# A two-by-two Strassen scheme for w1, and two quadrants added up in PSUM

## The chip, the cores and the metric

The kernel runs on all 8 cores of one Trainium2 chip, each on its own 2048 rows of the input with the same weights; the cores exchange nothing. The time is the device time of the slowest core, in microseconds (us).

## The reference, cut to what matters

```python
xn = _layernorm(x, axis=-1)                       # x: 16384 rows of 1024
s = _L0_attn_ref(xn, input_weights, xis, proj_matrix)
# inside the feed-forward part; _tlin(x, w, s) is (x @ w.T) * s
h = jax.nn.silu(_tlin(x, w1_w, w1_s)) * _tlin(x, w2_w, w2_s)     # 1024 -> 4096, twice
h = jax.nn.gelu(_tlin(h, h1_w, h1_s), approximate=False)         # 4096 -> 4096
h = jax.nn.gelu(_tlin(h, h2_w, h2_s), approximate=False)         # 4096 -> 4096
g = _silu(_tlin(h, w3_w, w3_s))                                  # 4096 -> 1024
x = x + s * g
```

The weights w1, w2, h1, h2 and w3 are ternary (-1, 0, 1); each output column has a scale.

## The kernel before, in words

**Passes and stages.** A core works through two passes (`s_` = 0, 1) of 1024 columns, where a column is one row of x, held transposed. A pass has the stages w12 (w1 and w2 with the gate), h1, h2 and w3; between the passes stands the attention part, which computes s for both. Activations lie in SBUF as bf16 in ten blocks `blk` of 16 tiles of 128 x 512; a tile is 128 features by half of the columns (`th` = 0, 1; N = 512).

**w12 before (`w12_stage`).** 32 chunks, each of 128 features of w1 and the same 128 of w2. For each `th`, `chunk` issues 8 matmuls of w1 into one PSUM bank and 8 of w2 into another, and `gate` has ScalarE write silu of the first to `stg` (L301) and VectorE multiply the second by its scale and by that (L306). Chunk `2*row + half` and `th` give quadrant (half+1, th+1) of the 4096 x 1024 product at `row`: quadrants 11, 12, 21, 22. After two chunks `sums` makes the five sums of quadrants that the next stage reads (L290 to L294). In the first pass `head0` interleaves the layernorm of the second 512 columns with chunks 0 to 6.

**h1, h2, w3 (`hidden_stage`, `row_group`).** These use Strassen's scheme with blocks named 11, 12, 21, 22: seven products M1 to M7 of 16 matmuls each, in the order M2, M5, M1, M4, M7, M3, M6 for each of 16 rows (4 in w3). Bank `bb` holds M2, then M4 is added on top; bank `ba` holds M5, then M3 on top. `ta` collects M1 - M2 - M5. VectorE adds: v1 = bank + ta (L421), then + M7 from a bank of its own (L428) is quadrant 11; v2 (L438), then + M6 from its own bank (L445) is quadrant 22. ScalarE's gelu (L492, L496) or silu follows each. The sums of weights (`weight_sums`, L369, and `sub_in_place`, L376) are made on VectorE during the row before and at the start of the row.

**What sets the order.** Each engine works strictly in the order in which the program issues. `need(engine, tokens)` is a wait; `V` and `S` wait for the instruction before on their own engine too. `take_bank` and `free_bank` hand the 8 PSUM banks round in the order in which they were freed, as the program is written. Weight tiles of 128 x 2048 go through a ring of 8 slots, `wring`; `plan` is the fixed order of loads ("L") and of slots for sums ("S"), and `give_slot` frees a slot once its last matmul is done, on which GpSimd issues the next load.

Of the kernel before, what the change touches and what calls it, by code (L numbers as in the profile page):

```python
# [36 lines left out]
def build_nc():  # L37
# [26 lines left out]
    with contextlib.ExitStack() as stack:  # L64
# [214 lines left out]
        def w12_stage(s_, xnb, bl, after_chunk, head, *toks):  # L279
# [4 lines left out]
            need(v, *toks)  # L284

            def sums(i):

                ops_ready["M2"] = [hv["11", i]]
                ops_ready["M5"] = [hv["22", i]]
                ops_ready["M1"] = [V(lambda: v.tensor_add(kt(bl["M1"], i), kt(h["11"], i), kt(h["22"], i)))]  # L290
                ops_ready["M4"] = [V(lambda: v.tensor_sub(kt(bl["M4"], i), kt(h["21"], i), kt(h["11"], i)))]
                ops_ready["M7"] = [V(lambda: v.tensor_add(kt(h["21"], i), kt(h["21"], i), kt(h["22"], i)))]
                ops_ready["M3"] = [V(lambda: v.tensor_sub(kt(bl["M3"], i), kt(h["12"], i), kt(h["22"], i)))]
                ops_ready["M6"] = [V(lambda: v.tensor_add(kt(h["12"], i), kt(h["12"], i), kt(h["11"], i)))]  # L294

            def gate(i, th, b1, m1, b2, m2):
                row, half = i // 2, i % 2
# [3 lines left out]
                a = S(lambda: sc.activation(stg[:, ts_, :], p[b1], AF.Silu,  # L301
                                            scale=w1s_c[:, oc:oc + 1]),
                      m1, gate_free.get(ts_), now(d_stg[ts_]), col_tok)
                free_bank(b1, a)
                q = str(half + 1) + str(th + 1)
# [36 lines left out]
            first, begun = head(chunk, head_chunks, gate) if head else (0, [])  # L342
            for i in range(first):
                ch = begun[i] if i < len(begun) else chunk(i, 1)
                gate(*ch)
                give_slot(key(i), ch[5])
                if i % 2 == 1:
                    sums(i // 2)
            for i in range(first, 32):
                for th in range(2):  # L350
                    ch = chunk(i, th)
                    gate(*ch)
                give_slot(key(i), ch[5])
                if i % 2 == 1:
                    sums(i // 2)
                after_chunk(i)
# [22 lines left out]
        def row_group(s_, nm, r, bl, nxt, emit, edge):  # L379
# [49 lines left out]
            free_bank(bd, a)  # L429
            t_free[2 * par + 1] = emit("11", r, tb, a)  # L430
# [143 lines left out]
        def head0(chunk, head_chunks, gate):  # L574
# [31 lines left out]
            return 7, ch  # L606

        xn_out = []
        xn_b = b_xn
        first_toks = [[], xn_out]  # L610
        for s_ in range(NS):
            last = s_ == NS - 1

            def after_chunk(i):
# [11 lines left out]
            if not last:  # L626
# [4 lines left out]
                def fetch_edge(u, m):  # L631
# [6 lines left out]
                    elif u == 4:  # L638
                        need(sy, end["u4"], *xn_out)
# [169 lines left out]
                ss = [f32b(b_x)[:, i, :] for i in range(8)] + [f32b(b_q)[:, i, :] for i in range(8)]  # L809
# [14 lines left out]
                first_toks = [[now(d) for d in d_y], [now(d_s)]]  # L824
# [132 lines left out]
```

How the kernel before makes its waits and increments, by code:

```python
    def inc(self, instr, k=1):  # L31
        instr.then_inc(self.sem, k)
        self.n += k
        return (self, self.n)
# [2 lines left out]
def build_nc():  # L37
# [78 lines left out]
        def need(eng, *toks):  # L116
            for tok in toks:
                if tok is None:
                    continue
                ctr, val = tok
                key = (id(eng), id(ctr))
                if val <= 0 or waited.get(key, 0) >= val:
                    continue
                eng.wait_ge(ctr.sem, val)
                waited[key] = val
# [763 lines left out]
                            load(4, [], [end["u6"]])  # L889
                        elif r in (1, 2) and u == 6:
                            load(4 * r + 4, [y_tok[n_] for n_ in range(4 * r - 4, 4 * r)], [])
                    return edge
                for r in range(4):
                    row_group(s_, "w3", r, bl, (s_, "w3", r + 1) if r < 3 else None, emit,
                              edge_load(r))
        for d in d_y:
            sy.wait_ge(d.sem, d.n)
    return nc
```

## Time and profile before

| what | value |
|---|---|
| median of 3 runs | 2374.67 us |
| the profiled execution, its own time | 2374.05 us |
| its span on the slowest core | 2373.0 us |
| TensorE busy, matmuls | 2348.3 us (99%), 10856 |
| VectorE busy | 1139.1 us (48%) |
| ScalarE busy | 416.7 us (18%) |
| mean granted TensorE clock | 0.998 |
| DMA, mean rate | 107 GB/s |

The busy time of an engine is the sum of its instructions; matmuls are pipelined, so that one lasts 379 ns in the records while the next begins some 216 ns after it. "Idle before <-X" is how long an engine stood still, and what X released it.

### The profile page before, as it was taken

The page shows a single profiled execution, that of the slowest core. Times are in us where ns is not written, and L with a number is a line of the kernel's source. Part 1 is how long each engine was busy: PE and PEld are TensorE (multiplying, and loading weights), DVE is VectorE, ACT ScalarE, POOL GpSimd, SP SyncE. Part 2 cuts the span into 40 slices and gives each one's busy share as a digit, 9 for nine tenths or more (in the row PEclk, how much of TensorE's full clock was granted, in tenths as well). Part 3 has the DMA queues.
Part 4 walks back from the last instruction along what each step waited for, and adds up shares of the span by engine and source line. Part 5 has one row for each costly group of instructions (what it writes and reads, how often), then busy time and mean ns, then how long its engine had stood idle before and what let it go on. Part 6 is the DMA issues. An engine that isn't in the chain of part 4 may idle for free.

```text
span 2373.0 us, 30116 instructions; the slowest of 8 cores (2369.7 to 2373.0 us)
## 1 busy us (share of the span) xinstructions
PE 2348.3 (99%) x10856; PEld 1062.3 (45%) x10856; DVE 1139.1 (48%) x1386; ACT 416.7 (18%) x589; POOL 227.9 (10%) x393
## 2 busy tenths in 40 slices
PE   7999999999999999999999999999999999999998
PEld 2444444444444444444444444444444444444443
DVE  4433444444644444463661333444444644444476
ACT  3211111111111111111623112111111111111111
POOL 1100000000100000012040000000000000000000
PEclk9999999999999999999999999999999999999999
DMA  7744456565765656598633443465565756565597
GB/s 108 134 81 71 76 87 107 87 110 91 150 104 95 105 90 111 87 194 136 117 107 103 75 80 63 76 98 102 93 108 89 155 93 108 89 108 92 102 195 201
DMA packets 92307, 253.70 MB, mean 107 GB/s; under 512 B 9856, under 2 KB 28416, under 8 KB 91904
## 3 DMA queue, kind: packets, MB, share of 16 engines
q0 software_dynamic: 57168, 192.96, 51.5%
q1 hardware_dynamic: 34992, 58.81, 7.9%
q8 instruction: 89, 1.46, 0.3%
q14 instruction: 58, 0.48, 0.1%
HBM read 415.31 MB, written 29.36 MB: 187 GB/s over the span
## 4 chain that ended last, share of the span: by engine, by line
PE 96%; DMA 2%; DVE 1%; ACT 0%; issue 0%; POOL 0%; DVEq 0%; ACTq 0%; POOLq 0%
PE pb L157 95%; DMA wring<-w3p 1%; PE pb L335 1%; DMA blk<-xT 0%; PE pb L234 0%; PE pb L235 0%; DVE blk L268 0%; DVE blk L262 0%; DVE blk L306 0%; DVE wring L369 0%; POOL blk L215 0%; DVE blk L860 0%; DVE blk L862 0%; ACT blk L256 0%; DVE blk L243 0%
## 5 line engine op out<-in xcount | busy, mean ns | idle before, releaser
L157 PE MATMUL pb<-blk,wring 128*128 128x512 bf16 x10016 | 2162.7, 379 | 4.5 <-DVE wring L369 2.0
L157 PEld LDWEIGHTS pb<-blk,wring 128*128 128x128 bf16 x10016 | 979.8, 98 | 1187.2 <-issue 6.4
L369 DVE TENSOR_TENSOR wring<-wring 128x2048 bf16<-128x2048 bf16 x216 | 264.6, 1225 | 50.1 <-DVE tmp L445 16.8
L306 DVE SCALAR_TENSOR_TENSOR blk<-pb,cols,stg 128x512 bf16<-128x512 f32 x128 | 96.1, 751 | 268.1 <-PE pb L157 222.0
L376 DVE TENSOR_TENSOR wring<-wring 128x2048 bf16<-128x2048 bf16 x144 | 176.4, 1225 | 15.0
L492 ACT ACTIVATE blk<-pb,cols 128x512 bf16<-128x512 f32 x64 | 44.0, 687 | 664.6 <-DVE tmp L421 664.6
L492 ACT ACTIVATE blk<-tmp,cols 128x512 bf16<-128x512 f32 x128 | 92.4, 722 | 344.0 <-DVE tmp L428 179.8
L301 ACT ACTIVATE stg<-pb,cols 128x512 bf16<-128x512 f32 x128 | 87.9, 687 | 338.4 <-PE pb L157 323.0
L445 DVE TENSOR_TENSOR tmp<-pb,tmp 128x512 f32<-128x512 f32 x72 | 49.8, 692 | 185.4 <-PE pb L157 185.2
L184 POOL DMA_DIRECT2D wring<-h1p x128 | 67.6, 528 | 740.4 <-PE pb L157 740.4
L157 PE MATMUL pb<-blk 128*128 128x512 bf16 x640 | 138.6, 379 | 0.0
L428 DVE TENSOR_TENSOR tmp<-pb,tmp 128x512 f32<-128x512 f32 x72 | 49.8, 692 | 179.3 <-PE pb L157 179.3
L184 POOL DMA_DIRECT2D wring<-h2p x128 | 67.7, 529 | 705.9 <-PE pb L157 673.5
L421 DVE TENSOR_TENSOR tmp<-pb,tmp 128x512 f32<-128x512 f32 x72 | 49.8, 692 | 171.6 <-PE pb L157 170.1
L414 DVE TENSOR_TENSOR tmp<-pb,tmp 128x512 f32<-128x512 f32 x72 | 49.8, 692 | 130.4 <-PE pb L157 129.2
L157 PEld LDWEIGHTS pb<-blk 128*128 128x128 bf16 x640 | 62.6, 98 | 75.5
L438 DVE TENSOR_TENSOR tmp<-pb,tmp 128x512 f32<-128x512 f32 x72 | 49.8, 692 | 88.5 <-PE pb L157 87.6
L496 ACT ACTIVATE stg<-pb,cols 128x512 bf16<-128x512 f32 x64 | 44.0, 687 | 173.4 <-DVE tmp L438 173.4
L184 POOL DMA_DIRECT2D wring<-w12p x64 | 34.2, 542 | 404.1 <-PE pb L157 348.5
L399 ACT COPY tmp<-pb 128x512 f32<-128x512 f32 x72 | 42.2, 586 | 143.9 <-PE pb L157 143.9
L408 DVE TENSOR_TENSOR tmp<-pb,tmp 128x512 f32<-128x512 f32 x72 | 49.8, 692 | 21.6 <-DVE wring L376 16.7
L681 DVE SCALAR_TENSOR_TENSOR tmp<-eb,cols,pb 128x512 f32<-128x512 bf16 x32 | 23.9, 747 | 23.4 <-ACT blk L685 13.8
(72 smaller groups left out, 522.6 us busy)
## 6 DMA issues: line engine op xcount, KB each, us to landing
wring<-h1p POOLq DMA_DIRECT2D x128, 512.0 KB, 7.4
wring<-h2p POOLq DMA_DIRECT2D x128, 512.0 KB, 7.7
wring<-w12p POOLq DMA_DIRECT2D x64, 512.0 KB, 5.9
wring<-w3p POOLq DMA_DIRECT2D x32, 512.0 KB, 10.3
blk<-xT SPq DMA_DIRECT2D x32, 256.0 KB, 8.1
y<-blk SPq DMA_DIRECT2D x32, 256.0 KB, 3.3
blk<-xT POOLq DMA_DIRECT2D x16, 256.0 KB, 22.9
s_hbm<-blk SPq DMA_DIRECT2D x16, 256.0 KB, 2.0
```

Of the source, the lines that this page charges most:

```text
L157: ii = t.matmul(p[bk], lhs, rhs, start=(not onto and i == 0), stop=(i == n - 1), skip_group_check=onto)
L184: toks = d_w[slot].inc(g.dma_start(wring[:, slot, :], src), 16)
L301: a = S(lambda: sc.activation(stg[:, ts_, :], p[b1], AF.Silu, scale=w1s_c[:, oc:oc + 1]), m1, gate_free.get(ts_), now(d_stg[ts_]), col_tok)
L306: a = V(lambda: v.scalar_tensor_tensor(kt(h[q], row), p[b2], w2s_c[:, oc:oc + 1], stg[:, ts_, :], op0=ALU.mult, op1=ALU.mult), m2, a)
L369: tok = V(lambda: v.tensor_add(wring[:, so, :], wring[:, slots[ka][0], :], wring[:, slots[kb][0], :]), *toks, slots[ka][1], slots[kb][1])
L376: tok = V(lambda: v.tensor_sub(wring[:, sa, :], wring[:, sa, :], wring[:, sb_, :]), *toks)
L408: rr = V(lambda: v.tensor_add(ta, p[ba], ta), m, a)
L414: vv = V(lambda: v.tensor_sub(ta, p[bc], ta), m, rr)
L421: v1 = V(lambda: v.tensor_add(tb, p[bb], ta), m, vv, t_free.get(2 * par + 1))
L428: a = V(lambda: v.tensor_add(tb, p[bd], tb), m, v1)
L438: v2 = V(lambda: v.tensor_add(ta, p[ba], ta), m, vv)
L492: a = S(lambda: sc.activation(dst, src, AF.Gelu, scale=s_col[:, oc:oc + 1]), tok, *first_tok)
```

## The change

w1 gets the scheme of the hidden layers: w1 and xn are cut in two by two, and a row (128 features of each half) has seven products of 4 matmuls each, while w2 stays at four plain groups of 8 on the quadrants. The first pass keeps rows 0 to 3 plain (`PLAIN`), the second has all 16 rows in the scheme. Five sums of xn (`input_sums`) and, for each row, five sums of weight tiles (`w12_weight_sums`, three into a slot of their own and two in place) are new work of VectorE. The sums for h1 are made for four rows at once (after rows 4, 8, 12 and 15 begin) and for row 15 at the end. In all layers with the scheme, M7 is now added in the bank of quadrant 21 and M6 in that of 12, after ScalarE has read these; v1 and v2 go, the order becomes M2, M5, M1, M4, M3, M7, M6, and `weight_sums` "s5" moves one unit ahead. The blocks that buffer s between the passes move to others.

```diff
+PLAIN = (4, 0)
...
             for i in range(32):
                 plan.append(("L", (s_, "w12", i, 0), w12p[i]))
+                if i % 2 == 1 and i // 2 >= PLAIN[s_]:
+                    plan.append(("S", (s_, "w12", i // 2, "sum"), None))
...
+        def input_sums(xnb, bl):
+            xn = wide(xnb)
+            b11, b12 = xn[:, 0:4, 0:N], xn[:, 0:4, N:2 * N]
+            b21, b22 = xn[:, 4:8, 0:N], xn[:, 4:8, N:2 * N]
+            at = lambda i: blk[:, bl["out11"] if i < 4 else bl["out22"],
+                               i % 4 * 2048:(i % 4 + 1) * 2048].rearrange("p (k c) -> p k c", k=4)
+            xs = {"M2": b11, "M5": b22, "M1": at(0), "M4": at(1), "M7": at(2), "M3": at(3), "M6": at(4)}
+            V(lambda: v.tensor_add(xs["M1"], b11, b22))
+            V(lambda: v.tensor_sub(xs["M4"], b21, b11))
+            V(lambda: v.tensor_sub(xs["M3"], b12, b22))
+            V(lambda: v.tensor_add(xs["M7"], b21, b22))
+            tok = V(lambda: v.tensor_add(xs["M6"], b11, b12))
+            return xs, tok
+        def w12_weight_sums(s_, r):
+            (sa, ta_), (sb, tb_) = slots[s_, "w12", 2 * r, 0], slots[s_, "w12", 2 * r + 1, 0]
+            so, toks = slots[s_, "w12", r, "sum"]
+            a11, a12 = wring[:, sa, 0:N], wring[:, sa, N:2 * N]
+            a21, a22 = wring[:, sb, 0:N], wring[:, sb, N:2 * N]
+            out = lambda i: wring[:, so, i * N:(i + 1) * N]
+            V(lambda: v.tensor_add(out(0), a21, a22), *toks, ta_, tb_)
+            V(lambda: v.tensor_add(out(1), a11, a12))
+            V(lambda: v.tensor_add(out(2), a11, a22))
+            V(lambda: v.tensor_sub(a12, a12, a22))
+            slots[s_, "w12", r, "sum"] = (so, V(lambda: v.tensor_sub(a21, a21, a11)))
...
+            def sums(i0, i1):
+                rows = lambda b: blk[:, b, i0 * N:(i1 + 1) * N]
+                ops_ready["M2"] = [hv["11", i1]]
+                ops_ready["M5"] = [hv["22", i1]]
+                ops_ready["M1"] = [V(lambda: v.tensor_add(rows(bl["M1"]), rows(h["11"]), rows(h["22"])))]
...
+            def row_plain(first):
+                ch = head(chunk, head_chunks, gate)
+                for i in range(first):
+                    c = ch[i] if i < len(ch) else chunk(i, 1)
+                    gate(*c)
+                    give_slot(key(i), c[5])
+                for i in range(first, 2 * PLAIN[s_]):
+                    for th in range(2):
+                        c = chunk(i, th)
+                        gate(*c)
+                    give_slot(key(i), c[5])
+            def row(r):
+                par = r % 2
+                ta, tb = tmp[:, 2 * par, :], tmp[:, 2 * par + 1, :]
+                ka, kb, ks = key(2 * r), key(2 * r + 1), (s_, "w12", r, "sum")
+                def unit(bk, kw, k0, op, onto=False):
+                    need(t, slots[kw][1])
+                    return mm_group(bk, [(wtile(kw, k0 + k), xs[op][:, k, :]) for k in range(4)], onto)
+                def plain(q):
+                    kw = kb if q[0] == "2" else ka
+                    cs = slice(0, N) if q[1] == "1" else slice(N, 2 * N)
+                    bk = take_bank()
+                    return bk, mm_group(bk, [(wtile(kw, 8 + k), xn[:, k, cs]) for k in range(8)])
+                bb = take_bank()
+                m = unit(bb, ks, 0, "M2")
+                copy_tok = S(lambda: sc.copy(ta, p[bb]), m, t_free.get(2 * par))
+                ba = take_bank()
+                m = unit(ba, ks, 4, "M5")
+                rr = V(lambda: v.tensor_add(ta, p[ba], ta), m, copy_tok)
+                if r < 15:
+                    w12_weight_sums(s_, r + 1)
+                z21 = plain("21")
+                bc = take_bank()
+                m = unit(bc, ks, 8, "M1")
+                give_slot(ks, m)
+                vv = V(lambda: v.tensor_sub(ta, p[bc], ta), m, rr)
+                free_bank(bc, vv)
+                for i0, i1 in ((0, 3), (4, 7), (8, 11), (12, 14)):
+                    if r == i1 + 1:
+                        sums(i0, i1)
+                z12 = plain("12")
+                need(t, copy_tok)
+                m = unit(bb, kb, 4, "M4", onto=True)
+                g21 = silu(1, r, p[bb], m)
+                z11 = plain("11")
+                need(t, rr)
+                m = unit(ba, ka, 0, "M3", onto=True)
+                g12 = silu(0, r, p[ba], m)
+                z22 = plain("22")
+                product("21", r, *g21, *z21)
+                after_row(r, 0)
+                product("12", r, *g12, *z12)
+                after_row(r, 1)
+                need(t, g21[1])
+                m = unit(bb, ka, 4, "M7", onto=True)
+                give_slot(ka, m)
+                a = V(lambda: v.tensor_add(tb, p[bb], ta), m, vv, t_free.get(2 * par + 1))
+                free_bank(bb, a)
+                g11 = silu(0, r, tb, a)
+                t_free[2 * par + 1] = g11[1]
+                need(t, g12[1])
+                m = unit(ba, kb, 0, "M6", onto=True)
+                give_slot(kb, m)
+                a = V(lambda: v.tensor_add(ta, p[ba], ta), m)
+                free_bank(ba, a)
+                g22 = silu(1, r, ta, a)
+                t_free[2 * par] = g22[1]
+                product("11", r, *g11, *z11)
+                product("22", r, *g22, *z22)
+                after_row(r, 2)
+            if head:
+                row_plain(7)
+                xs, xs_tok = input_sums(xnb, bl)
+                w12_weight_sums(s_, PLAIN[s_])
+            else:
+                xs, xs_tok = xs
+            need(t, xs_tok)
+            for r in range(PLAIN[s_], 16):
+                row(r)
+            sums(15, 15)
...
             m = unit(bb, "a22", "M4", onto=True)
             give_slot(key("a22"), m, slots[key("a12")][1])
-            v1 = V(lambda: v.tensor_add(tb, p[bb], ta), m, vv, t_free.get(2 * par + 1))
-            free_bank(bb, emit("21", r, p[bb], v1))
+            out21 = emit("21", r, p[bb], m)
             edge_(3, m)
-            bd = take_bank()
-            m = unit(bd, "a12", "M7")
-            give_slot(key("a12"), m)
-            a = V(lambda: v.tensor_add(tb, p[bd], tb), m, v1)
-            free_bank(bd, a)
-            t_free[2 * par + 1] = emit("11", r, tb, a)
+            need(t, rr)
+            m = unit(ba, "a11", "M3", onto=True)
+            give_slot(key("a11"), m, slots[key("a21")][1])
+            out12 = emit("12", r, p[ba], m)
             if nxt:
                 weight_sums(*nxt, "s2")
             edge_(4, m)
-            need(t, rr)
-            m = unit(ba, "a11", "M3", onto=True)
-            give_slot(key("a11"), m, slots[key("a21")][1])
-            v2 = V(lambda: v.tensor_add(ta, p[ba], ta), m, vv)
-            free_bank(ba, emit("12", r, p[ba], v2))
+            need(t, out21)
+            m = unit(bb, "a12", "M7", onto=True)
+            give_slot(key("a12"), m)
+            a = V(lambda: v.tensor_add(tb, p[bb], ta), m, vv, t_free.get(2 * par + 1))
+            free_bank(bb, a)
+            t_free[2 * par + 1] = emit("11", r, tb, a)
+            if nxt:
+                weight_sums(*nxt, "s5")
             edge_(5, m)
-            be = take_bank()
-            m = unit(be, "a21", "M6")
+            need(t, out12)
+            m = unit(ba, "a21", "M6", onto=True)
             give_slot(key("a21"), m)
-            a = V(lambda: v.tensor_add(ta, p[be], ta), m, v2)
-            free_bank(be, a)
+            a = V(lambda: v.tensor_add(ta, p[ba], ta), m)
+            free_bank(ba, a)
             t_free[2 * par] = emit("22", r, ta, a)
             if nxt:
-                weight_sums(*nxt, "s5")
...
-                if i >= 29:
-                    weight_sums(s_, "h1", 0, ("s2", "s5", "s1")[i - 29])
-            w12_stage(s_, xn_b, bl, after_chunk, None if s_ else head0, *first_toks[0])
+            def after_row(r, i):
+                if r == 15:
+                    weight_sums(s_, "h1", 0, ("s2", "s5", "s1")[i])
...
-                ss = [f32b(b_x)[:, i, :] for i in range(8)] + [f32b(b_q)[:, i, :] for i in range(8)]
+                ss = [f32b(fr2)[:, i, :] for i in range(8)] + [f32b(fr1)[:, i, :] for i in range(8)]
+                bl = {"M2": b_sq, "M5": b_wt, "M1": b_f, "M4": fr1, "M7": fr2, "M3": fr3,
+                      "M6": b_iw, "out11": b_x, "out22": b_q, "out21": b_xn1}
+                xs_next = input_sums(b_xn1, bl)
+                w12_weight_sums(1, 0)
...
-                first_toks = [[now(d) for d in d_y], [now(d_s)]]
-                bl = {"M2": b_sq, "M5": b_wt, "M1": b_f, "M4": fr1, "M7": fr2, "M3": fr3,
-                      "M6": b_iw, "out11": b_x, "out22": b_q, "out21": b_xn1}
+                first_toks = [[now(d) for d in d_y] + [now(d_s)], []]
...
-                order = [(("21", "11", "12", "22")[k], r) for r in range(4) for k in range(4)]
+                order = [(("21", "12", "11", "22")[k], r) for r in range(4) for k in range(4)]
...
-                            load(0, [end["u4"]], [end["u5"], now(d_s)])
+                            load(0, [end["u5"]], [now(d_s)])
```

## Rows read from the trace of the kernel before

**Rows 1.** waits of TensorE, whole span: total us, times, longest

```profile
PE pb L335 <- DVE blk L268: 6.1, 1, 6.1
...
PE pb L157 <- DVE wring L369: 2.0, 2, 1.3
...
PE pb L157 <- ACT stg L301: 1.6, 1, 1.6
```

**Rows 2.** windows of h1 and the second w12, columns in its first line

```profile
core 6: us, PE busy (x) PEld busy (x) DVE busy (x) ACT busy (x) POOL busy (x), PEclk, DMA share, GB/s
257.00:644.00 387.00, 387.00 (x1795) 175.45 (x1794) 186.83 (x211) 55.74 (x81) 33.83 (x64) 1.00 0.61 104
...
1273.00:1495.00 222.00, 222.00 (x1031) 100.64 (x1029) 81.77 (x141) 45.84 (x66) 14.84 (x28) 1.00 0.40 69
```

**Rows 3.** the chain that ended last: start us, length us, what

```profile
22.78 7.18 PE pb L335 x24
...
1054.58 1.24 DVE wring L369
1055.81 0.14 issue
...
1190.79 1087.81 PE pb L157 x5040
```

**Rows 4.** windows of 2 us around TensorE's longest idle time

```profile
16.00:18.00 2.00, 0.67 (x4) 0.10 (x1) 1.12 (x2) 0.44 (x1) 0.00 (x0) 1.00 1.06 160
18.00:20.00 2.00, 0.00 (x0) 0.00 (x0) 1.72 (x3) 0.44 (x2) 0.00 (x0) 0.93 1.01 152
...
24.00:26.00 2.00, 2.00 (x6) 0.76 (x5) 1.90 (x2) 0.00 (x0) 0.00 (x0) 0.50 1.11 145
26.00:28.00 2.00, 2.00 (x9) 0.83 (x8) 1.79 (x3) 1.18 (x2) 0.00 (x0) 0.87 1.27 171
```

**Rows 5.** groups by form, VectorE and ScalarE: busy us, mean ns | idle before

```profile
L369 DVE TENSOR_TENSOR wring<-wring 128x2048 bf16<-128x2048 bf16 x216 | 264.6, 1225 | 50.1 <-DVE tmp L445 16.8 <-DVE tmp L428 16.4 <-DMA wring<-w3p 8.1
...
L306 DVE SCALAR_TENSOR_TENSOR blk<-pb,cols,stg 128x512 bf16<-128x512 f32 x128 | 96.1, 751 | 268.1 <-PE pb L157 222.0 <-ACT stg L301 35.0 <-DVE blk L294 6.8
...
L301 ACT ACTIVATE stg<-pb,cols 128x512 bf16<-128x512 f32 x128 | 87.9, 687 | 338.4 <-PE pb L157 323.0 <-PE pb L335 11.7 <-DVE blk L290 2.8
...
L408 DVE TENSOR_TENSOR tmp<-pb,tmp 128x512 f32<-128x512 f32 x72 | 49.8, 692 | 21.6 <-DVE wring L376 16.7 <-PE pb L157 5.0
...
L262 DVE TENSOR_TENSOR blk<-blk 128x1024 f32<-128x1024 bf16 x8 | 9.8, 1225 | 0.8
...
L290 DVE TENSOR_TENSOR blk<-blk 128x512 bf16<-128x512 bf16 x32 | 13.6, 425 | 3.3
```

**Rows 6.** timeline of VectorE, first w12: start us, length us, what

```profile
45.65 0.75 DVE L306 SCALAR_TENSOR_TENSOR blk<-pb,cols,stg 128x512 bf16<-128x512 f32 x1 [0.17 <-DVE blk L306]
...
245.59 0.75 DVE L306 SCALAR_TENSOR_TENSOR blk<-pb,cols,stg 128x512 bf16<-128x512 f32 x1 [0.24 <-PE pb L157]
...
254.30 0.75 DVE L306 SCALAR_TENSOR_TENSOR blk<-pb,cols,stg 128x512 bf16<-128x512 f32 x1 [2.70 <-PE pb L157]
255.15 0.42 DVE L290 TENSOR_TENSOR blk<-blk 128x512 bf16<-128x512 bf16 x1
255.68 0.43 DVE L291 TENSOR_TENSOR blk<-blk 128x512 bf16<-128x512 bf16 x1
```

**Rows 7.** DMA issues of the page: KB, median us to landing

```profile
wring<-h1p POOLq DMA_DIRECT2D x128, 512.0 KB, 7.4
...
wring<-w12p POOLq DMA_DIRECT2D x64, 512.0 KB, 5.9
wring<-w3p POOLq DMA_DIRECT2D x32, 512.0 KB, 10.3
```

**Rows 8.** timeline of VectorE, end of the program

```profile
2367.39 0.69 DVE L445 TENSOR_TENSOR tmp<-pb,tmp 128x512 f32<-128x512 f32 x1 [0.17 <-DVE blk L862]
...
2369.87 0.69 DVE L862 TENSOR_TENSOR blk<-blk 128x512 f32<-128x512 f32 x1
```

More of the change, by code:

```diff
@@ L276, in ln_extra, with w12_stage @@
                                              op0=ALU.mult, op1=ALU.mult), ln[th, "rstd"])
-        def w12_stage(s_, xnb, bl, after_chunk, head, *toks):
+        def input_sums(xnb, bl):
[22 more added lines that the diff above has]
+            slots[s_, "w12", r, "sum"] = (so, V(lambda: v.tensor_sub(a21, a21, a11)))
+        def w12_stage(s_, xnb, bl, xs, after_row, head, *toks):
             xn = wide(xnb)
@@ L283, in w12_stage, with silu @@
             gate_n = [0]
[L284 to L297, printed above, removed]
+            def sums(i0, i1):
[3 more added lines that the diff above has]
+                ops_ready["M1"] = [V(lambda: v.tensor_add(rows(bl["M1"]), rows(h["11"]), rows(h["22"])))]
+                ops_ready["M4"] = [V(lambda: v.tensor_sub(rows(bl["M4"]), rows(h["21"]), rows(h["11"])))]
+                ops_ready["M3"] = [V(lambda: v.tensor_sub(rows(bl["M3"]), rows(h["12"]), rows(h["22"])))]
+                ops_ready["M7"] = [V(lambda: v.tensor_add(rows(h["21"]), rows(h["21"]), rows(h["22"])))]
+                ops_ready["M6"] = [V(lambda: v.tensor_add(rows(h["12"]), rows(h["12"]), rows(h["11"])))]
+            def silu(half, row, src, tok):
                 oc = half * 16 + row
@@ L300, in gate, with product @@
                 gate_n[0] += 1
[L301 to L305, printed above, removed]
+                return ts_, S(lambda: sc.activation(stg[:, ts_, :], src, AF.Silu,
+                                                    scale=w1s_c[:, oc:oc + 1]),
+                              tok, gate_free.get(ts_), now(d_stg[ts_]), col_tok)
+            def product(q, row, ts_, a, b2, m2):
+                oc = (int(q[0]) - 1) * 16 + row
                 a = V(lambda: v.scalar_tensor_tensor(
                     kt(h[q], row), p[b2], w2s_c[:, oc:oc + 1], stg[:, ts_, :],
-                    op0=ALU.mult, op1=ALU.mult), m2, a)
+                    op0=ALU.mult, op1=ALU.mult), m2, a, *toks)
                 gate_free[ts_] = a
@@ L311, in gate @@
                 hv[q, row] = a
+            def gate(i, th, b1, m1, b2, m2):
+                row, half = i // 2, i % 2
+                ts_, a = silu(half, row, p[b1], m1)
+                free_bank(b1, a)
+                product(str(half + 1) + str(th + 1), row, ts_, a, b2, m2)
             key = lambda i: (s_, "w12", i, 0)
@@ L340, in head_chunks @@
                         for i in range(n)] if jj == 3 else None
[L342 to L356, printed above, removed]
+            def row_plain(first):
[9 more added lines that the diff above has]
+                    give_slot(key(i), c[5])
@@ L605, in head0 @@
             xn_out.append(d_xn.inc(sy.dma_start(xn_hbm, blk[:, b_xn, :]), 16))
-            return 7, ch
+            return ch
         xn_out = []
         xn_b = b_xn
+        xs_next = None
         first_toks = [[], xn_out]
@@ L612, in build_nc @@
             last = s_ == NS - 1
-            def after_chunk(i):
-                if i >= 29:
-                    weight_sums(s_, "h1", 0, ("s2", "s5", "s1")[i - 29])
-            w12_stage(s_, xn_b, bl, after_chunk, None if s_ else head0, *first_toks[0])
+            def after_row(r, i):
+                if r == 15:
+                    weight_sums(s_, "h1", 0, ("s2", "s5", "s1")[i])
+            w12_stage(s_, xn_b, bl, xs_next, after_row, None if s_ else head0, *first_toks[0])
             bl = hidden_stage(s_, "h1", bl, h1s_c, "h2", first_toks[1])
@@ L638, in fetch_edge @@
                     elif u == 4:
-                        need(sy, end["u4"], *xn_out)
+                        need(sy, end["u5"], *xn_out)
                         fetched["xn"] = d_xn.inc(sy.dma_start(blk[:, fr3, :], xn_hbm), 16)
```

## The prediction

> **What bounds the kernel now.** I read the waits of TensorE first: the whole span holds few, and the longest (6.1 us) lie in the layernorm of the head; of the long middle there is 2.0 us for sums of w3's weights [rows 1]. Then the windows by stage: TensorE is busy for all 387.0 us of h1 and for all 222.0 us of the second w12, at a clock of 1.00 [rows 2]. Then the chain that ended last, which names one piece of 1087.81 us with 5040 matmuls, 0.2158 us each [rows 3]. So the time is the number of matmuls times 0.2158 us plus holes, and any hole that the change opens in front of TensorE counts in full. VectorE has room today: 81.77 of 222 us, 37%, in w12 [rows 2].
>
> **What it removes.** A row of w1 and w2 costs 64 matmuls today (two halves, two `th`, 16 each) and 7*4 + 4*8 = 60 then. There are 12 such rows in the first pass and 16 in the second: 28*4 = 112 matmuls, 112*0.2158 = **24.2 us less**, if they run back to back. A row then lasts 60*0.2158 = 12.95 us. In the hidden layers the count stays; 144 adds of VectorE go (v1 and v2, 72 rows, 0.69 us each by the like of [rows 5]), some 100 us of its work, but TensorE never waited for them there: nothing.
>
> **What it adds: a hole after the plain rows.** In the first pass `input_sums` stands behind the last plain gate in VectorE's order, and `row(4)` can't begin before it and before `w12_weight_sums`. Nothing is queued for TensorE meanwhile. Price: the last product 0.75 [rows 5] and its start, 0.8; five adds of 2048 bf16 elements, for which the nearest row is the weight sum of the same size, 1.225 [rows 5], and 0.10 to the next one (425 ns long, 0.53 from start to start [rows 6]), 5*1.33 = 6.65; five adds of 512, 5*0.53 = 2.65; 0.14 to TensorE [rows 3]. Together **10.3 us**. The operands of `input_sums` are four runs of 512 and not one run of 2048: if that halves the rate, as for the float32 centering that takes 1225 ns for 1024 elements [rows 5], an add takes 2.29 us and the hole is 5.3 us longer. I take the fast figure since the inner run is contiguous as in the rows at 425 ns. The Trainium skill (VectorE: DVE Perf Modes, What auto-detection actually checks) asks for 16-bit tensors with a step of one for the double rate; by it the hole stays at 10.3 us, and no row here has this very form.
>
> **And the clock.** Before the 6.1 us wait of today the clock was 1.00; the window 18:20 shows a mean of 0.93, so it fell near 19.9, and it came back in 26:28 (0.87), some 3.5 us after the matmuls had restarted at 22.78 (the figure before the last two of each window's line is the clock, columns as in [rows 2]) [rows 4]. The 24 matmuls there took 7.18 us [rows 3] where 24*0.2158 is 5.18: the fall costs **2.0 us**. The new hole is longer, so I add it once in full.
>
> **A hole before h1, in both passes.** h1's first product needs quadrant 11 of row 15, which today is long done. In the new order VectorE makes it after both late adds. I count from the start of row 15, from the durations in [rows 5] with the lags of [rows 6] (0.17 before one that reads PSUM behind another, 0.24 behind or before a weight sum): the row before leaves an add and two products, so rr ends at 3.45; vv follows M1 (4.32) and ends at 5.1; the sums of rows 12 to 14 are five adds of 1536 (0.96 each, between 425 for 512 and 1225 for 2048) with 0.10 between, to 10.4; product 21 to 11.4; s2 of h1 to 12.9; product 12 to 13.8; s5 to 15.3; the add after M7 to 16.3; that after M6 to 17.1; product 11 to 18.1; TensorE at 18.2. It had finished at 12.95: **5.25 us, twice, 10.5 us**. Product 22, s1 and the last sums follow under M2's 3.45 us and M5's. Bounds: 3.5 us each if the lags are smaller and s5 comes ahead of its turn, 7 if a load holds s5. Does the clock fall in 5.25 us? The only fall known is at 6.1 us; I take half of 2.0 for each, **2.0 us** together, with 0 and 4.0 as bounds. The Trainium skill (TensorE: Matmul & The Clock Gate, Why this matters for your kernels) warns of idle gaps between bursts; it would have the clock fall in all three holes, which makes 4.0 of these 2.0.
>
> **Small waits inside the rows.** Each row takes 7 of 8 banks, so a bank is needed again one row later. In rows 4, 8 and 12 of the program VectorE has five adds of 2048 more: rr to 3.45, weight sums to 6.2, vv to 7.2, the stage sums to 13.8, product 21 to 14.8, and its bank is wanted at 12.95 + 1.73 = 14.7. I take 0.3 us, six times, **2 us**; 0 and 9 us are the bounds (below). In other rows VectorE catches up.
>
> **What is hidden.** The second pass's `input_sums` and first weight sums (9.3 us) run under the 128 matmuls of s (27.6 us). M7 now waits for ScalarE to have read quadrant 21, and M6 for 12: some 0.7 us each [rows 5], and a table load once in a stage, under 16 matmuls of 3.45 us. "s5" is now wanted 10.4 us after its load is issued, which lands in 7.4 us in h1 [rows 7]; where it is later (w3, 10.3 us) VectorE stands, with the add after M6 behind it, but TensorE needs s5 only 3.45 us later, and that wait is today's 2.0 us [rows 1]. The loads of w12 are issued some 16 us before their sums and land in 5.9 us [rows 7]. Fetches and spills keep their place by units. At the end, VectorE starts its last PSUM add at 2367.39, held up by the add before it, and ends at 2370.56 [rows 8]; with one add less it is some **0.3 us** earlier.
>
> **Sum.** 2374.05 - 24.2 + 10.3 + 2.0 + 10.5 + 2.0 + 2 - 0.3 = 2376.4 for the profiled execution; the median of the runs is 0.6 above that execution, so **2377 us**, 0.1% more than today. A measurement of this kernel can tell about 2% from no change.
>
> **Rivals.**
> (1) *The holes are covered*: the sums run ahead of where I place them, and only the matmuls count: 2374.7 - 24.2 = 2350 us. For it: VectorE is 63% idle in w12. Against: its order is the program's, and a product of the last plain chunk stands in front of the sums. 0.07.
> (2) *VectorE paces the w1 rows*, the case on the slower side. Its work per row with lags: rr 0.9, weight sums 2.9, vv 0.9, four products 3.7, two adds 1.7, a quarter of the stage sums 1.7, together 11.8 of 12.95 us, 91% instead of 37%. It decides from 0.07 us more for each of the 16 instructions of a row on. Then the six bank waits grow from 0.3 to some 1.5 us (+7) and each hole before h1 by 1 us (+2): 2386. If the bf16 adds ran at half rate in all places, each row would be 1.4 us over: 28 of them and the longer hole give 2420; the 425 ns rows speak against that. 0.18.
> (3) *The input sums run at half rate and the clock falls in all three holes*: 2377 + 5.3 + 2 = 2384 us. For it: the strided form is not in the trace. Against: the contiguous runs of 512. 0.12.
> The forecast, the holes as priced, has 0.60; 0.03 is for something that I don't see, more likely slower.
>
> **Range.** Low end: small lags (-3.5), no fall of the clock before h1 (-2) nor after the plain rows (-2), no bank waits (-2), a little of the first hole: 2366. High end: rivals (2) and (3) with most of their price: 2390. It leaves out rival (1) and the tails, under 0.15. Faster by over 2% would need 47 us, which no case gives: 0.01; slower by as much only the extreme form of (2): 0.03; within 2% 0.96.
>
> **What would show it.** TensorE: 10744 matmuls instead of 10856; one wait of some 10 us before the first scheme row, near 88 us, for a VectorE weight sum, with the clock at half behind it; one of some 5 us before h1 at about 257 and 1491 us for a product of VectorE; waits of a few tenths for bank releases three times in each w12; none within h1 and h2. Input sums at 1.23 us (or 2.29, rival 3). VectorE's share in the second w12 near 75%. I am wrong if the waits before h1 are absent or TensorE waits in every row.

## The result, and the profile after

The changed kernel takes 2380.17 us (median of 12 undisturbed executions) against 2374.78 us (14): ratio 1.0022, 95% interval 1.0014 to 1.003, so 5.4 us slower and within 2%. The forecast was 2377 us, 2366 to 2390. The profiled execution took 2378.95 us, its span is 2377.9 us on core 4. Disturbed executions, in which the cores of a die ran at a lower granted clock, are left out of all medians and ratios here (with them the two medians are 2380.64 and 2374.9 us); on one chip some at 20 us above the rest stayed in and made three intervals wide, where the profiles are the better reading. The kernels ran on several chips, and the kernel before has medians of 2374.24 to 2374.84 us on them, so a difference between kernels of two chips is good to some 0.6 us.

The page of the changed kernel, its engines and two of its groups of instructions (busy us, mean ns of one | idle before them):

```profile
PE 2332.0 (98%) x10744; PEld 1052.1 (44%) x10744; DVE 1170.8 (49%) x1394; ACT 435.2 (18%) x617; POOL 229.3 (10%) x393
...
L158 PE MATMUL pb<-blk,wring 128*128 128x512 bf16 x9904 | 2145.3, 380 | 27.2 <-DVE blk L338 12.5
...
L338 DVE SCALAR_TENSOR_TENSOR blk<-pb,cols,stg 128x512 bf16<-128x512 f32 x128 | 96.1, 751 | 71.2 <-ACT stg L332 35.4
```

TensorE has 10744 matmuls instead of 10856. Its busy time fell by 16 us and not by the 24.2 us of 112 matmuls, since some of the others now run at a lowered clock, as shown below. VectorE has 32 us more, though 144 adds went from the hidden layers. The idle time of TensorE ahead of its main group is 27.2 us; it was 4.5 us on the page of the kernel before.

The waits of TensorE in the changed kernel answer to [rows 1]:

```profile
PE pb L158 <- DVE blk L338: 12.5, 7, 5.7
PE pb L158 <- DVE wring L309: 10.5, 1, 10.5
PE pb L373 <- DVE blk L271: 6.1, 1, 6.1
...
PE pb L158 <- DVE wring L478: 1.5, 2, 1.2
```

The first two are new: 12.5 us for products of VectorE (L338 is `product` and `gate`) in seven waits, and 10.5 us in one piece for the last of the weight sums (L309). In the timeline of TensorE each stretch without a wait is one line; the bracket is the wait before it:

```profile
67.12 20.88 PE L158 MATMUL pb<-blk,wring 128*128 128x512 bf16 x96
98.51 68.56 PE L158 MATMUL pb<-blk,wring 128*128 128x512 bf16 x308 [10.50 <-DVE wring L309]
167.69 4.48 PE L158 MATMUL pb<-blk,wring 128*128 128x512 bf16 x20 [0.62 <-DVE blk L338]
172.35 47.64 PE L158 MATMUL pb<-blk,wring 128*128 128x512 bf16 x220 [0.18 <-issue]
220.26 37.34 PE L158 MATMUL pb<-blk,wring 128*128 128x512 bf16 x172 [0.27 <-DVE blk L338]
262.73 803.02 PE L158 MATMUL pb<-blk,wring 128*128 128x512 bf16 x3712 [5.12 <-DVE blk L338]
...
1284.47 66.64 PE L158 MATMUL pb<-blk,wring 128*128 128x512 bf16 x308
1351.38 52.02 PE L158 MATMUL pb<-blk,wring 128*128 128x512 bf16 x240 [0.28 <-DVE blk L338]
1403.67 52.02 PE L158 MATMUL pb<-blk,wring 128*128 128x512 bf16 x240 [0.27 <-DVE blk L338]
1455.96 37.35 PE L158 MATMUL pb<-blk,wring 128*128 128x512 bf16 x172 [0.27 <-DVE blk L338]
1498.96 802.77 PE L158 MATMUL pb<-blk,wring 128*128 128x512 bf16 x3712 [5.65 <-DVE blk L338]
```

The reader finds here the hole after the plain rows (10.50 us), the holes before h1 (5.12 and 5.65 us) and six waits of 0.18 to 0.62 us within w12. No line breaks inside h1 or h2: 3712 matmuls follow one another. A record shows a matmul as 0.38 us long while the next starts 0.216 us after it, so each wait is 0.16 us longer than its bracket says: 96 matmuls at 0.2158 us are 20.72 us, the record of the first line has 20.88.

VectorE in the first hole, from its timeline (start us, length us):

```profile
88.18 0.75 DVE L338 SCALAR_TENSOR_TENSOR blk<-pb,cols,stg 128x512 bf16<-128x512 f32 x1 [2.70 <-PE pb L158]
89.04 1.23 DVE L291 TENSOR_TENSOR blk<-blk 128x2048 bf16<-128x2048 bf16 x1
...
97.94 0.42 DVE L309 TENSOR_TENSOR wring<-wring 128x512 bf16<-128x512 bf16 x1
```

The last plain product (L338) is followed by the five input sums (L291 to L295), each 1.22 or 1.23 us long, and by the five weight sums (L305 to L309), each 0.42 us long. VectorE's load over most of the second w12 answers to the second line of [rows 2], in the same columns:

```profile
1285.00:1492.00 207.00, 206.18 (x954) 92.75 (x952) 143.83 (x219) 54.63 (x80) 15.98 (x30) 1.00 0.46 78
```

It is busy for 143.83 of 207 us, 69%, where it was 37% before.

The clock after the first hole, in windows of 2 us (columns as in [rows 2], the clock third from the end; they answer to [rows 4]):

```profile
90.00:92.00 2.00, 0.00 (x0) 0.00 (x0) 1.79 (x3) 0.00 (x0) 0.00 (x0) 1.00 0.88 131
92.00:94.00 2.00, 0.00 (x0) 0.00 (x0) 1.90 (x2) 0.00 (x0) 0.00 (x0) 0.55 0.73 104
98.00:100.00 2.00, 1.49 (x4) 0.58 (x5) 0.36 (x1) 0.00 (x0) 0.00 (x0) 0.50 0.00 0
102.00:104.00 2.00, 2.00 (x10) 0.85 (x9) 1.40 (x3) 0.00 (x0) 0.00 (x0) 0.89 0.04 8
260.00:262.00 2.00, 0.00 (x0) 0.00 (x0) 1.55 (x3) 0.96 (x2) 0.00 (x0) 1.00 0.97 133
262.00:264.00 2.00, 1.27 (x4) 0.56 (x5) 1.72 (x3) 0.48 (x1) 0.00 (x0) 0.71 0.66 129
...
266.00:268.00 2.00, 2.00 (x10) 0.94 (x9) 1.69 (x4) 0.00 (x0) 0.00 (x0) 0.93 0.00 0
```

It fell in the hole near 92 and came back after 102; before h1 it fell at about 262.8, just as the wait ended, and came back after 266, and near 1498.5, in the hole before the second h1, once more. Thus 308 matmuls after the first hole lasted 68.56 us where the same stretch takes 66.64 us at full clock (the experiment with the input sums in the head has it), 1.9 us more. The stretch of 3712 matmuls behind the second hole took 803.02 us against 801.33 us at full clock (seen in the experiments with z22 last and with the filled holes), 1.7 us more, and behind the third 802.77, 1.4 us more.

VectorE before the third hole, from its timeline (start us, length us, idle before):

```profile
1489.83 0.96 DVE L326 TENSOR_TENSOR blk<-blk 128x1536 bf16<-128x1536 bf16 x1
1490.96 0.75 DVE L338 SCALAR_TENSOR_TENSOR blk<-pb,cols,stg 128x512 bf16<-128x512 f32 x1 [0.17 <-DVE blk L326]
1491.95 1.23 DVE L478 TENSOR_TENSOR wring<-wring 128x2048 bf16<-128x2048 bf16 x1 [0.24 <-DVE blk L338]
1493.42 0.75 DVE L338 SCALAR_TENSOR_TENSOR blk<-pb,cols,stg 128x512 bf16<-128x512 f32 x1 [0.24 <-PE pb L158]
1494.41 1.23 DVE L478 TENSOR_TENSOR wring<-wring 128x2048 bf16<-128x2048 bf16 x1 [0.24 <-DVE blk L338]
1496.16 0.69 DVE L441 TENSOR_TENSOR tmp<-pb,tmp 128x512 f32<-128x512 f32 x1 [0.53 <-DVE wring L478]
1497.03 0.69 DVE L448 TENSOR_TENSOR tmp<-pb,tmp 128x512 f32<-128x512 f32 x1 [0.17 <-DVE tmp L441]
1498.06 0.75 DVE L338 SCALAR_TENSOR_TENSOR blk<-pb,cols,stg 128x512 bf16<-128x512 f32 x1 [0.34 <-ACT stg L332]
```

This is the chain that the prediction worked out: the last stage sum, product 21, s2, product 12, s5, the adds behind M7 and M6, product 11. TensorE had finished w12 by 1493.3 us and waits for the last of these lines.

### The profile page after: what moved, and what is told of

Read it like the earlier page. It is cut to its first block, busy times and chain, and to the rows that moved or that the text cites. A ratio compares the mean times of both kernels' runs of the same rounds, so it can differ in the third digit from the quotient of the medians.

```text
span 2377.9 us, 30054 instructions; the slowest of 8 cores (2374.2 to 2377.9 us)
## 1 busy us (share of the span) xinstructions
PE 2332.0 (98%) x10744; PEld 1052.1 (44%) x10744; DVE 1170.8 (49%) x1394; ACT 435.2 (18%) x617; POOL 229.3 (10%) x393
## 4 chain that ended last, share of the span: by engine, by line
PE 92%; DVE 4%; DMA 2%; issue 1%; ACT 0%; DVEq 0%; POOL 0%; ACTq 0%; POOLq 0%
PE pb L158 91%; DMA wring<-w3p 1%; PE pb L373 1%; DVE blk L338 1%; DMA blk<-xT 0%; DVE blk L322 0%; DVE blk L326 0%; DVE blk L323 0%; DVE blk L325 0%; DVE blk L324 0%; PE pb L237 0%; PE pb L238 0%; DVE wring L478 0%; DVE blk L271 0%; DVE blk L265 0%
## 5 line engine op out<-in xcount | busy, mean ns | idle before, releaser
L158 PE MATMUL pb<-blk,wring 128*128 128x512 bf16 x9904 | 2145.3, 380 | 27.2 <-DVE blk L338 12.5
L158 PEld LDWEIGHTS pb<-blk,wring 128*128 128x128 bf16 x9904 | 969.1, 98 | 1203.1 <-issue 41.5
L545 DVE TENSOR_TENSOR tmp<-pb,tmp 128x512 f32<-128x512 f32 x72 | 49.8, 692 | 365.5 <-PE pb L158 364.6
L523 DVE TENSOR_TENSOR tmp<-pb,tmp 128x512 f32<-128x512 f32 x72 | 49.8, 692 | 171.0 <-PE pb L158 170.1
L338 DVE SCALAR_TENSOR_TENSOR blk<-pb,cols,stg 128x512 bf16<-128x512 f32 x128 | 96.1, 751 | 71.2 <-ACT stg L332 35.4
L555 DVE TENSOR_TENSOR tmp<-pb,tmp 128x512 f32<-128x512 f32 x72 | 49.8, 692 | 85.2 <-PE pb L158 84.2
L517 DVE TENSOR_TENSOR tmp<-pb,tmp 128x512 f32<-128x512 f32 x72 | 49.8, 692 | 74.8 <-PE pb L158 73.1
L332 ACT ACTIVATE stg<-pb,cols 128x512 bf16<-128x512 f32 x72 | 49.5, 687 | 191.0 <-PE pb L158 178.4
L605 ACT ACTIVATE stg<-pb,cols 128x512 bf16<-128x512 f32 x64 | 44.0, 687 | 177.2 <-PE pb L158 177.2
L332 ACT ACTIVATE stg<-tmp,cols 128x512 bf16<-128x512 f32 x56 | 40.4, 722 | 111.0 <-DVE tmp L441 106.6
L791 DVE SCALAR_TENSOR_TENSOR tmp<-eb,cols,pb 128x512 f32<-128x512 bf16 x32 | 23.9, 748 | 24.5 <-ACT blk L795 15.7
L795 ACT ACTIVATE blk<-tmp,bias_f,cols 128x512 bf16<-128x512 f32 x32 | 26.0, 813 | 45.5 <-DVE tmp L791 45.4
## 6 DMA issues: line engine op xcount, KB each, us to landing
wring<-w3p POOLq DMA_DIRECT2D x32, 512.0 KB, 10.3
```

Source lines behind the costliest of these rows:

```text
L158: ii = t.matmul(p[bk], lhs, rhs, start=(not onto and i == 0), stop=(i == n - 1), skip_group_check=onto)
L332: return ts_, S(lambda: sc.activation(stg[:, ts_, :], src, AF.Silu, scale=w1s_c[:, oc:oc + 1]), tok, gate_free.get(ts_), now(d_stg[ts_]), ...
L338: a = V(lambda: v.scalar_tensor_tensor(kt(h[q], row), p[b2], w2s_c[:, oc:oc + 1], stg[:, ts_, :], op0=ALU.mult, op1=ALU.mult), m2, a, *toks)
L517: rr = V(lambda: v.tensor_add(ta, p[ba], ta), m, a)
L523: vv = V(lambda: v.tensor_sub(ta, p[bc], ta), m, rr)
L545: a = V(lambda: v.tensor_add(tb, p[bb], ta), m, vv, t_free.get(2 * par + 1))
```

## The experiments

Kernels that ran together share their runs of the kernel before; ratios are to that.

### Input sums in the head

```diff
             ln_extra(1)
+            early.append(input_sums(b_xn, bl))
             need(sy, ln[1, "xn", 3])
...
                         c = chunk(i, th)
+                        if (i, th) == (2 * PLAIN[s_] - 1, 1):
+                            w12_weight_sums(s_, PLAIN[s_])
                         gate(*c)
...
-                xs, xs_tok = input_sums(xnb, bl)
-                w12_weight_sums(s_, PLAIN[s_])
+                xs, xs_tok = early[0]
```

> The five sums of xn are made in the head, right after the layernorm of the second 512 columns, and the first weight sums ahead of the last plain gate. Theory (each hole in front of TensorE counts in full, and the clock falls behind it): the wait of 10.5 us for a weight sum goes, and the 2.1 us of half clock behind it, so 12.6 us less than the changed kernel: 2368 us, ratio to the kernel before 0.997. Rival (the hole is only moved: the sums now hold up the gates of chunks 0 to 2, banks run short in the head): half of it comes back, 2374 us, ratio 1.000, with a new wait of TensorE between 60 and 75 us.

Measured: 2368.24 us, ratio 0.9981 (0.9965 to 0.9998). The timeline of TensorE in this kernel, at the same places:

```profile
67.69 20.88 PE L158 MATMUL pb<-blk,wring 128*128 128x512 bf16 x96
88.98 66.64 PE L158 MATMUL pb<-blk,wring 128*128 128x512 bf16 x308 [0.40 <-DVE wring L309]
```

The hole shrank from 10.50 to 0.40 us, the 308 matmuls behind it take 66.64 us, and nothing new stands in the head. Against the 2380.2 us of the changed kernel that is 11.9 us; 12.6 were expected. The hole was a matter of order alone.

### Row 15 reordered

```diff
-                for i0, i1 in ((0, 3), (4, 7), (8, 11), (12, 14)):
+                for i0, i1 in ((0, 3), (4, 7), (8, 11), (12, 13)):
...
+                if r == 15:
+                    after_row(r, 0)                  # s2 of h1
+                    product("21", r, *g21, *z21)
...                                                   # M7, its add, M6, its add, as before
+                    z22 = plain("22")
+                    product("11", r, *g11, *z11)
+                    product("22", r, *g22, *z22)
+                    after_row(r, 1)                  # s5
+                    product("12", r, *g12, *z12)
+                    after_row(r, 2)                  # s1
+                    return
...
-            sums(15, 15)
+            sums(14, 15)
```

> Only row 15 of w12 is reordered: z22 is issued last on TensorE, h1's first weight sum comes before product 21, s5 behind product 22, and the stage sums of rows 12 and 13 are made in row 14, those of 14 and 15 at the end. Theory: the waits of 5.1 and 5.7 us before h1 fall under 0.5 us each and the clock no longer falls there (2.1 us each): some 14 us less than the changed kernel, 2366 us, ratio 0.996. Rival (VectorE has too much work at this place, and TensorE meets the same backlog some units later, at h1's M3, which needs an add of VectorE): 2372 us, ratio 0.999, with waits of some 2 us within h1's first row.

Measured: 2366.41 us, ratio 0.9997 (0.997 to 1.0024). Of the nine executions six lie at 2365.5 to 2366.7 us, among them the profiled one (2366.41), and three at 2386.4 to 2386.7. The ratio is inconclusive, the profile is not: TensorE's stretch from row 13 into h1, h2 and up to w3 is now one line in each pass.

```profile
220.38 839.04 PE L158 MATMUL pb<-blk,wring 128*128 128x512 bf16 x3884 [0.27 <-DVE blk L338]
...
1449.58 839.04 PE L158 MATMUL pb<-blk,wring 128*128 128x512 bf16 x3884 [0.62 <-DVE blk L338]
```

3884 matmuls at 0.2158 us are 838.3 us, so there is neither a wait nor a lowered clock of more than 0.6 us in them. The median of the lower six, 2365.9 us, is 14.3 us under the changed kernel; 14 were expected. The backlog does not come back within h1's first row.

### The holes filled with matmuls

```diff
+            def keep_busy(n):
+                i, tok = banks.popleft()
+                need(t, tok)
+                for _ in range(n):
+                    t.matmul(p[i], ones_d, xn[:, 0, 0:N], start=True, stop=True)
+                banks.appendleft((i, None))
...
                 row_plain(7)
+                keep_busy(46)
...
+            keep_busy(22)
             sums(15, 15)
```

> The changed kernel with matmuls that compute nothing of use in its three holes: 46 after the plain rows (9.9 us) and 22 before each h1 (4.7 us). The holes keep their length. Theory (the 6.4 us that the sum of matmuls, waits and holes leaves over is the clock at half behind each hole): the clock stays at 1.00 outside the head, 6.3 us less than the changed kernel, 2374 us, ratio 1.000. Rival (what is left over lies in the hidden layers or in w12's rows, and the lowered clock is only shown, not paid): 2380 us, ratio 1.002.

Measured: 2373.9 us, ratio 1.0011 (0.9979 to 1.0043), which can't tell 6 us, so the kernel ran again beside the changed one:

> The changed kernel itself, on the same chip as the next kernel, since the filled holes left an interval of 0.9979 to 1.0043 that can't tell 6 us. Both theories: ratio 1.0022 to the kernel before, 2380 us.

Measured: 2380.46 us, ratio 1.0022 (1.0012 to 1.0033).

> The kernel with the three holes filled by matmuls once more, beside the changed kernel. Theory (the clock at half behind the holes costs 5.2 to 6.3 us in all): 2374.5 us, 6 us less than the changed kernel, mean clock 0.998 on all cores against 0.994. Rival (the lowered clock is shown, not paid): the same time as the changed kernel within 1 us.

Measured: 2374.24 us, ratio 0.9998 (0.9989 to 1.0008); the intervals don't touch. The clock in the windows of the first filled kernel:

```profile
88.00:98.00 10.00, 9.70 (x45) 4.21 (x43) 8.82 (x11) 0.00 (x0) 0.53 (x1) 1.00 0.31 52
98.00:104.00 6.00, 5.73 (x27) 2.67 (x28) 2.96 (x8) 0.58 (x1) 0.00 (x0) 1.00 0.00 0
...
258.00:263.00 5.00, 4.63 (x23) 1.94 (x21) 4.27 (x6) 1.44 (x2) 0.00 (x0) 1.00 0.60 105
```

The waits for VectorE's results ended when they did before (0.57 us of wait behind 9.9 us of added matmuls, where 10.50 us of wait stood), only the clock stayed at 1.00. So some 6.2 us of the changed kernel's time (2380.46 - 2374.24) are the lowered clock. One core's records give 1.9 + 1.7 + 1.4 = 5.0 us; the time of eight cores is that of the slowest, and the falls differ from core to core (the 308 matmuls behind the first hole took 68.0 to 69.5 us on the eight cores of the repeated run).

### The two halves of the change apart

The first kernel is the one before with `row_group` of the changed one (and the waits at the passages that go with it), the second the changed one with `row_group` of before.

> The kernel before with the second half of the change alone: M7 and M6 are added up in the banks of 21 and 12 in h1, h2 and w3, w12 stays plain. Theory (TensorE never waited for the adds that go, and the new waits for ScalarE are covered by a unit of 3.45 us): ratio 1.000, within 1 us of the kernel before, some 100 us less work on VectorE. Rival (the new waits for ScalarE and the earlier s5 cost TensorE something in each of 72 rows): 5 us more, ratio 1.002.

Measured: 2373.26 us, ratio 0.9994 (0.9985 to 1.0004). VectorE's busy time fell from 1139.1 to 1038.4 us:

```profile
PE 2337.0 (99%) x10639; PEld 1062.5 (45%) x10856; DVE 1038.4 (44%) x1242; ACT 416.7 (18%) x589; POOL 228.4 (10%) x393
```

The count of TensorE has missing records here (10639 of 10856). A hundred microseconds of VectorE went, and the time did not move by what can be told.

> The changed w12, with the hidden layers as they were (M7 and M6 in banks of their own, order M2, M5, M1, M4, M7, M3, M6). Theory: w12 alone makes the whole difference to the kernel before, and the two halves add up: 2374.5 + 6 from w12, some 1 us above the changed kernel, 2381 us, ratio 1.003. Rival (w12 profits from the banks that the hidden layers no longer take, or the two disturb each other at the passage to h1): the wait before h1 differs by over 1 us from the 5.1 and 5.7 us of the changed kernel.

Measured: 2380.84 us, ratio 1.0026 (1.0015 to 1.0038), with waits of 10.50, 5.13 and 5.29 us. w12 alone makes the difference, and (2380.84 - 2374.41) + (2373.26 - 2374.24) is 5.5 us, near the 5.4 us of both: the halves add up.

### Stage sums split over two rows

```diff
                     if r == i1 + 1:
-                        sums(i0, i1)
+                        sums(i0, i1, 0 if i1 < 12 else 2)     # 0: M1, M4, M3
+                    elif r == i1 + 2 and i1 < 12:
+                        sums(i0, i1, 1)                       # 1: M7, M6
```

> The five stage sums of four rows are made in two rows: M1, M4, M3 in rows 4, 8, 12 and M7, M6 one row later. Theory (the waits of 0.27 to 0.62 us for a product of VectorE are bank waits caused by the 6.65 us of sums before it): these go, holes as before, 1.9 us less than the changed kernel, 2379 us, ratio 1.0015. Rival (they come from VectorE's average load, not from the lump): they stay or move to the next row, 2380.6 us.

Measured: 2377.83 us, ratio 1.0014 (1.0002 to 1.0025). TensorE runs the whole of the second w12 in one line:

```profile
1284.54 207.36 PE L158 MATMUL pb<-blk,wring 128*128 128x512 bf16 x960
```

The waits within w12 are gone, in the first pass too (one stretch of 720 matmuls there), and with them the one of 0.18 us that the record puts to no one. The 2.3 us by the medians is within what two intervals leave open; that the waits are gone is seen.

### Two adds more in each row

```diff
             V(lambda: v.tensor_add(out(0), a21, a22), *toks, ta_, tb_)
+            V(lambda: v.tensor_add(out(0), a21, a22))
             V(lambda: v.tensor_add(out(1), a11, a12))
+            V(lambda: v.tensor_add(out(1), a11, a12))
```

> The changed kernel with two of the five weight sums of each w1 row made twice: two adds of 512 elements, 1.06 us of VectorE, more in each of 28 rows. Theory (VectorE is 90% busy there but has room except behind the stage sums): the six bank waits grow by 1.05 us each, the hole after the plain rows by 1.06 us: 7.4 us more, 2388 us, ratio 1.0055. Rival (VectorE already paces the rows, as I held possible): each of the rows pays 1.06 us, 28 us more, 2409 us, ratio 1.0145.

Measured: 2387.0 us, ratio 1.0052 (1.0032 to 1.0072). The waits within the second w12 (some matmuls are missing from the counts):

```profile
1357.10 51.80 PE L158 MATMUL pb<-blk,wring 128*128 128x512 bf16 x235 [1.33 <-DVE blk L340]
1410.45 52.01 PE L158 MATMUL pb<-blk,wring 128*128 128x512 bf16 x236 [1.55 <-DVE blk L340]
1463.79 37.34 PE L158 MATMUL pb<-blk,wring 128*128 128x512 bf16 x168 [1.33 <-DVE blk L340]
```

This is core 6, where the changed kernel shows 0.27, 0.49 and 0.27 us at these places (some records are missing on core 6 of both kernels; cores with all of them show 1.33 us against 0.27). Each grew by the 1.06 us added, the two waits for products in the first pass likewise (1.32 and 1.33 us), the hole after the plain rows went from 10.50 to 11.56 us, and no other row waits. By the medians it is 6.8 us more than the changed kernel; 7.4 were expected, 28 by the rival. VectorE is close to pacing these rows, but does so only behind the lump of stage sums.

### Two steps of the reorder alone

In the first kernel s5 is called after product 22 in row 15. In the second z22 is last on TensorE as above, but the stage sums of rows 12 to 14 stay in row 15 and s2 behind product 21.

> Of the reorder of row 15 only one step: h1's weight sum s5 goes behind product 22 in both passes. Theory (the wait before h1 is VectorE's queue, each entry at its full length): the waits shrink by 1.5 and 1.8 us to 3.6 and 3.8 us. If the clock still falls behind them: 3.3 us less than the changed kernel, 2377 us, ratio 1.001. If it no longer falls: 7.5 us less, 2373 us, ratio 0.999. Rival (the wait is set by something else, such as silu of quadrant 11): waits unchanged, 2380.6 us.

Measured: 2377.78 us, ratio 1.001 (0.9998 to 1.0022); waits of 3.65 and 4.01 us.

> In row 15 the plain group z22 is issued last on TensorE, and s5 and product 12 come behind product 22; the stage sums of rows 12 to 14 stay in row 15 and s2 stays behind product 21. Theory by VectorE's queue: the add after M7 starts 13.1 us into the row, product 11 ends at 15.6, TensorE finished at 12.95: waits of 2.8 us, no fall of the clock, 9 us less than the changed kernel, 2372 us, ratio 0.9985. Rival (eight matmuls at the end cover the whole queue, as in the full reorder): waits under 0.5 us, 2366 us, ratio 0.996.

Measured: 2372.24 us, ratio 0.999 (0.998 to 1.0001); waits of 2.44 and 2.60 us. Both fit VectorE's queue within 0.4 us. On the clock I was wrong: behind 2.44 us it fell on two of the eight cores, and behind 2.60 us on four. Windows of cores 1 and 6 of the second kernel, the same stretch:

```profile
259.00:261.00 2.00, 0.54 (x2) 0.28 (x3) 1.59 (x3) 1.07 (x2) 0.09 (x1) 0.89 0.63 61
261.00:263.00 2.00, 2.00 (x6) 0.66 (x5) 1.65 (x3) 0.00 (x0) 0.00 (x0) 0.50 1.00 201
```

```profile
259.00:261.00 2.00, 0.98 (x5) 0.51 (x6) 1.50 (x2) 0.72 (x1) 0.00 (x0) 1.00 0.58 84
261.00:263.00 2.00, 2.00 (x11) 0.87 (x9) 1.79 (x2) 0.00 (x0) 0.00 (x0) 1.00 0.90 178
```

The 3712 matmuls behind it took 803.02 us on core 1 and 801.33 us on core 6. With s5 late, too, core 7 kept its full clock behind the wait of 4.01 us while core 6 lost it. The time is that of the slowest core, and so near the 2377 us expected for s5 late with falls, not the 2373 us without.

### All three mends together

> The early sums of xn, the reordered row 15 and the split stage sums together. Theory: what is left is 112 matmuls less and about 1.1 us from the hidden layers, with under 1 us of waits: 2374.5 - 24.2 - 1.1 + 1 = 2350 to 2353 us, ratio 0.990. Rival (the parts share a gain, as where VectorE's work put off in one place fills another): under two thirds of it, 2358 us or more, ratio over 0.993.

Measured: 2350.53 us, ratio 0.9899 (0.9882 to 0.9916): 23.9 us less than the kernel before, clock 0.997 to 0.998 on all cores. Waits of TensorE, then its timeline from the second w12 to the end:

```profile
PE pb L375 <- DVE blk L271: 6.1, 1, 6.1
...
PE pb L158 <- DVE wring L507: 0.9, 1, 0.9
PE pb L158 <- DVE wring L309: 0.4, 1, 0.4
```

```profile
1264.95 1078.13 PE L158 MATMUL pb<-blk,wring 128*128 128x512 bf16 x4992
```

The second pass runs from w12 to the last matmul, 4992 of them, without a wait. The parts were worth 11.9, 14.3 and 2.3 us alone, 28.5 in sum, and 29.6 us together: no gain is shared that the medians could tell.

## Why the prediction was right, point by point

- **Matmuls, -24.2 us.** Held: 10744, and units of four on changing banks ran at 0.2158 us each like all others. The version with all mends gains 23.9 us, which is this term and little else.
- **The hole after the plain rows, 10.3 us.** 10.50 by the record. Its five sums took 1.23 us each, the fast figure; the half-rate part of rival 3 is out. The rule of the Trainium skill (VectorE: DVE Perf Modes, What auto-detection actually checks) fits these rows: 16-bit tensors in runs with a step of one, at 1.23 us for 2048 elements and not 2.29.
- **The clock after it, 2.0 us.** 1.9. The 2.0 was read from a record that is itself 0.16 us too long, so the fall in the head had cost 1.8.
- **The holes before h1, 10.5 us.** 5.12 and 5.65, so 10.8. That VectorE's queue sets them is shown by taking entries out of it in steps (with s5 late 3.65 and 4.01, with z22 last 2.44 and 2.60, in the whole reorder none). Of the second hole's extra 0.5 us, 0.53 instead of 0.17 us before the add behind M7 and 0.34 instead of 0.17 before product 11 are seen in the timeline; the latter is a wait for ScalarE's silu, and what held the add back is open.
- **The clock before h1, 2.0 us for both.** This is the term that was mis-sized: it fell in both holes, on every core of the profiled execution, 1.7 + 1.4 us on core 4, and all three falls cost 6.2 us by the medians where I had 4.0. I had priced a 5 us hole at half because the one known fall stood at 6.1 us; it falls behind shorter ones as well. The warning of the Trainium skill (TensorE: Matmul & The Clock Gate, Why this matters for your kernels) was the better guide here, and rival 3 was right in this half.
- **Bank waits, 2 us.** 1.9 us in six waits. Five of them are behind the three lumps of sums in each pass as worked out, less the first row of the scheme, which has no backlog before it; a sixth, of 0.18 us, the record puts to no one, but it goes with the others when the sums are split.
- **What was not in the sum.** Each of the nine new waits costs 0.16 us more than its bracket, some 1.4 us. The waits for w3's weights were 0.5 us shorter and the head 0.4 us earlier, neither of which I traced further. The terms give -24.2 + 10.5 + 1.9 + 10.8 + 3.1 + 1.9 + 1.4 - 0.5 - 0.4 = +4.5 us; the spans differ by 4.9. The forecast had +2.3 for the same two executions. Of the 2.6 us between, 1.4 are the brackets and 1.1 the clock before h1; the other misses are of a few tenths each and of both signs, and they nearly cancel.
- **The tail, -0.3 us.** Not there: the last PSUM add starts 0.97 us after the last matmul in both kernels, [rows 8] and 2372.26 after 2371.29, since the two pairs of `finish` (L972, L974) still stand in front of it.
- **Hidden parts.** The waits for ScalarE in h1, h2 and w3 and the earlier s5 cost nothing, shown by the half alone; the second pass's input sums left no wait before its w12.
- **Rivals.** (1) was not what happened, though a reordered program gets exactly its 2350 us. (2) VectorE does not pace the rows; its price was tested by adding 1.06 us a row, which five bank waits and the hole after the plain rows paid and the other rows did not. Its busy share in the second w12 is 69%, where I had named some 75% as a sign.

## What to carry to other kernels

When one engine is busy 99% of the time, work taken from it is paid in full only if the helper's queue is read at the seams: price the first row, the last row and the passage to the next stage by listing what stands in front of the result that is awaited, entry by entry. A lump of helper work that costs some 0.3 us in the middle of a stage can cost nearly its whole length at the seam (s5, an add of 1.23 us, was worth 1.5 and 1.6 us of wait there), and moving it by a few lines of program order got back nearly all of it here. A hole of a few microseconds in TensorE's stream also costs the lowered clock behind it, some 2 us each in this kernel, so several short holes can be worse than one long.

## What the runs showed of the hardware that I had not expected

Behind waits of 2.44 us, and still of 3.65 and 4.01 us, the granted clock fell to half on some cores and stayed full on others of the same execution; behind those of 5.12 us and more it fell on all eight. A fall cost between 1.3 and 2.9 us. Useless matmuls put into a wait of fixed length saved 6.2 us of 2380.5, although they computed nothing. Adding up in a bank that ScalarE has just read cost nothing that could be told in 144 places.
